# Two of VectorE's phases in a four-bit feed-forward stage change places

## The reference

```python
def fp4_quant_dequant(x):
    xb = x.reshape(shape[:-1] + (shape[-1] // BLOCK, BLOCK))          # BLOCK = 16
    scale = jnp.max(jnp.abs(xb), axis=-1, keepdims=True) / 6.0
    scale = jnp.maximum(scale, jnp.float32(1e-12))
    xn = xb / scale
    idx = jnp.searchsorted(_MID, jnp.abs(xn))
    q = _GRID[idx] * jnp.sign(xn) * scale
    return q.reshape(shape)

gate = fp4_linear(x, w_gate)
y = fp4_linear(x, w_up)
h = jax.nn.silu(gate) * y
return fp4_linear(h, w_down)
```

## Time and profile before

| | us |
|---|---|
| three runs: lowest, median, highest | 2645.53, 2656.07, 2657.33 |
| the profiled execution: its span | 2660.2 |
| of it TensorE busy | 2396.7 (90%) |
| VectorE busy | 1794.1 (67%) |
| ScalarE busy | 1297.3 (49%) |
| GpSimd busy | 710.9 (27%) |
| mean granted TensorE clock | 0.944 of full speed |

### The profile page before, as it was taken

How to read it: one execution, slowest core, us unless ns; L and a number is a source line. 1 busy time by engine, 2 the same in 40 slices (tenths; PEclk the granted TensorE clock), 3 DMA queues, 4 the chain that set the end, 5 groups by cost and what they waited for, 6 DMA issues and landing times. The chain is left out here.

```text
span 2660.2 us, 43690 instructions
## 1 busy us (share of the span) xinstructions
PE 2396.7 (90%) x15960; PEld 2204.5 (83%) x15960; DVE 1794.1 (67%) x3357; ACT 1297.3 (49%) x2026; POOL 710.9 (27%) x468
## 2 busy tenths in 40 slices
PE   6988896798999978999999999993999999499999
PEld 6887885788888877988988898883899999399998
DVE  5566665899999966566566566544667765777774
ACT  4344443334433324464454455444566665356555
POOL 1011011444444433123123023113244441211111
PEclk9999997899999998999999999975999999699999
DMA  5000000000000000000000000002000010000000
GB/s 171 0 0 0 0 0 18 2 1 0 0 0 0 1 1 17 13 8 12 16 4 12 16 6 9 16 9 64 17 24 24 16 48 1 34 19 30 24 24 32
DMA packets 42971, 45.69 MB, mean 17 GB/s; under 512 B 3088, under 2 KB 41872, under 8 KB 42640
## 3 DMA queue, kind: packets, MB, share of 16 engines
q1 hardware_dynamic: 42896, 44.69, 5.1%
HBM read 27.90 MB, written 16.78 MB: 17 GB/s over the span
## 5 line engine op out<-in xcount | busy, mean ns | idle before, releaser
L1842 DVE TENSOR_TENSOR m_a_lo<-m_a,m_a_hi 128x512 fp32r<-128x512 f32 x128 | 107.3, 839 | 126.4 <-ACT m_a_hi L1800 126.4
L1796 ACT ACTIVATE d_a<-d_ps_wide,d_b,d_w_gain 128x512 f32<-128x512 f32 x128 | 100.1, 782 | 136.7 <-PE d_ps_wide L271 134.4
L1269 POOL TENSOR_TENSOR p_kf<-p_kf,p_k_shift 128x1024 f32<-128x1024 f32 x64 | 119.4, 1904 | 155.4 <-DVE p_k_shift L1403 155.4
L1755 PE MATMUL m_ps_z<-m_w_hi,m_a_hi 128*128 128x256 f32 x512 | 147.4, 288 | 9.2 <-DVE m_w_lo L1821 9.2
L1796 ACT ACTIVATE m_a<-m_ps_wide,m_b 128x512 f32<-128x512 f32 x128 | 88.0, 688 | 121.3 <-PE m_ps_wide L271 121.2
L1755 PE MATMUL m_ps_z<-m_w_hi,m_a_lo 128*128 128x256 f32 x512 | 145.6, 284 | 0.0
L1755 PE MATMUL m_ps_z<-m_w_lo,m_a_hi 128*128 128x256 f32 x512 | 145.3, 284 | 0.0
L1755 PE MATMUL d_ps_z<-d_w_hi,d_a_hi 128*128 128x256 f32 x512 | 143.6, 280 | 1.1 <-DVE d_a_lo L1842 1.1
L1755 PE MATMUL d_ps_z<-d_w_lo,d_a_hi 128*128 128x256 f32 x512 | 143.4, 280 | 0.0
L1755 PE MATMUL d_ps_z<-d_w_hi,d_a_lo 128*128 128x256 f32 x512 | 142.6, 278 | 0.0
L1842 DVE TENSOR_TENSOR d_a_lo<-d_a,d_a_hi 128x512 fp32r<-128x512 f32 x128 | 85.8, 689 | 77.1 <-ACT d_a_hi L1800 72.5
(11 more groups left out here) (361 smaller groups left out, 8580.1 us busy)
## 6 DMA issues: line engine op xcount, KB each, us to landing
residual<-in_x SPq DMA_DIRECT2D x8, 1024.0 KB, 11.8
attn<-p_attn SPq DMA_DIRECT2D x32, 256.0 KB, 2.1
m_attn<-attn SPq DMA_DIRECT2D x16, 512.0 KB, 3.7
out<-residual SPq DMA_DIRECT2D x16, 512.0 KB, 2.9
raw_weights<-in_d_q SPq DMA_DIRECT2D x2, 1024.0 KB, 7.1
d_scale<-in_d_scale SPq DMA_DIRECT2D x2, 1024.0 KB, 5.3
raw_weights<-in_m_w1T SPq DMA_DIRECT2D x1, 1024.0 KB, 5.1
raw_weights<-in_m_w2T SPq DMA_DIRECT2D x1, 1024.0 KB, 7.5
```

The lines of the kernel that those rows point to most:

```text
L1269: pool.tensor_tensor(f, f, k_shift[:, i, :].unsqueeze(2).broadcast_to([P, HEADS, M]), ALU.subtract).then_inc(k_shifted, 1)
L1755: mm = pe.matmul(z, a, w[:, f, :], start=(f == 0 and k == 0 and j % 2 == 0), stop=(f == FC - 1 and k == 2), skip_group_check=True)
L1796: act.activation(self.a[f % RING][:, :], self.ps_wide[f % 2][:, :], self.func, bias=self.b1[:, f:f + 1], scale=gain(f))
L1842: dve.tensor_tensor(self.a2[1][:, f, :], self.a[f % RING][:, :], self.a2[0][:, f, :].bitcast(F32), ALU.subtract).then_inc(self.a_lo, 1)
```

## The change

In VectorE's list of phases the block scales of the next normalised tile and the second gate product change places. Nothing else is touched.

```diff
             pipeline(dve, N, [(8, add_down), (4, split_n), (7, split_h(0)), (3, round_n), (6, round_h), (5, multiply(0)),
-                              (7, split_h(1)), (2, scales_n), (5, multiply(1)), (5, scales_h)], SLOTS)
+                              (7, split_h(1)), (5, multiply(1)), (2, scales_n), (5, scales_h)], SLOTS)
```

## The result

The changed kernel took 2680.89 us (median of 4 runs, 2673.06 to 2691.84) against 2650.94 us of the kernel before (four runs, 2645.53 to 2657.33): the ratio estimated from the runs is **1.0107**, 95% interval 1.0069 to 1.0145. It is slower by 30 us; the forecast was 38.6 us more and a time of 2695, with a range from 2675 to 2714. The 2695 started from 2656.07, the median of three runs; with the fourth run the median of the kernel before is 5 us lower. The profiled execution took 2685.33 us and has a span of 2683.6.

A forecast was written before the change was run, and what follows sets the result against it. Two close limits, VectorE and a loop through the other engines with 0.92 us to spare, bound the kernel; scales in the loop (+21.0 us) plus 12 clock falls (17.6) gave +38.6 us, 2695 us, range 2675 to 2714.

The forecast's parts named there:

- The two close limits: Four-bit stage, kernel before: VectorE's own queue, 15.66 us a step, and a loop through other engines with 0.92 us to spare.
- the collision: VectorE's small product for the normalised tile's scales, blocked by GpSimd's restoring: 1.00 us instead of 0.18, 0.82 us a step.
- the loop: Gate product's scales through GpSimd's division, ScalarE's first SiLU and TensorE's up product back to VectorE: 14.79 us by itself.
- The wait at the gate product: VectorE's second gate product waits for TensorE's up product: from 0 to 1.65 us in an ordinary step.
- The price of the scales in the loop: Normalised tile's scales between up product and gate product's scales add 0.73 + 0.65 + 0.34 = 1.72 us a step.
- The signal gap behind the reciprocal: VectorE, from the reciprocal's end of the normalised tile's scales to the next instruction: 0.34 us, low bound 0.04.
- The uncontended small product: VectorE's small product in the normalised tile's scales, clear of GpSimd's restoring: 0.18 us, 0.65 to the reciprocal's end.
- The first step: Start of the stage's first counted gate-product scales, whose product already waited for TensorE: 1.72 us later.
- The falls of the clock: TensorE's clock falling to 1.2 GHz in 12 of 28 steps instead of 8, 1.47 us each, 17.6 us.
- The sum: Whole forecast: +19.3 us in 28 steps, 1.72 for the first start, 17.6 for falls: +38.6 us.
- VectorE is the bound: Rival, faster: collision's 0.82 us saved each step, 2633 us, if the up product is done when the split ends; chance 0.02.

The follow-up runs named there:

- the filled kernels: Unread TensorE matmuls added to each step where TensorE waits: ten in the changed kernel, ratio 1.0030; nine in the kernel before, ratio 0.9994.

## Why the prediction was right

**What bounds the kernel.** The two close limits were there. With the collision taken away VectorE's 15.66 became 14.84 and stopped at the loop's 14.79; with the scales in the loop the step became 16.13. The rows that told it were the last three steps, not the busy share.

**The wait at the gate product.** Forecast 0 to 1.65 us in every step; measured in all 28, in the step shown 1.46 us (from the split's end at 746.37 to 747.83), and some 3 us in a step with a fall.

**The price of the scales in the loop: 1.72 us, measured 1.34** (16.13 - 14.79). Two pieces of this term were too large. The signal gap behind the reciprocal is 0.16 us, not 0.34: I took over the gap ahead of a product with three waits, and now one wait stands there. That the number of waits makes the difference was not tested. And the reduction starts 0.81 us after the gate product, not 0.93 (748.64 against 747.83), since it waits for nothing of it. That makes 0.30; the way from the scales to the up product, 13.70 us against 13.78 in the last steps, makes the rest. The uncontended small product was right: 0.18, and 0.65 to the reciprocal's end; the rule of the Trainium skill (SBUF — State Buffer, "Who interferes with whom") held in every order tried: 0.18 us wherever GpSimd was free, 0.54 to 1.28 wherever it was not, and 0.46 instead of 0.21 for the gate product's small product in the one kernel where that met GpSimd.

**The first step.** Forecast 1.72 us, measured 2.33 - 0.92 = 1.41, for the same reason.

**The falls of the clock: 12 expected, 18 measured.** The direction was right, and the filled kernels show the cause that was argued. The size was a choice between two ends and was too low; 18 lies on the edge of the 5 to 18 that the forecast allowed, so that it came out inside is luck. Its price of 1.47 us was right (1.53).

**The sum.** In the 28 steps +19.3 without falls and 17.6 for them were forecast, 36.9; measured 8.68 (451.68 - 443.00) and 27.66 (479.34 - 451.68), together 36.34. So the stage came out as forecast because two terms were off in opposite directions by 10 us each, not because both were known: that is luck. The kernel's 30 us are less than the stage's 36 to 38: the stages that the edit does not touch differ between executions, by 7.8 and 6.7 us in the two profiled ones, and four runs of each do not average that out. On record are 46 later runs of the kernel before; they lie between 2634.9 us (granted clock 0.954) and 2663.1 (0.944). Which stages make this spread is not shown.

**The rivals.** "VectorE is the bound" had the right price and fell on its condition: the up product did not end with the split. Of the orders tried, only the one with GpSimd's order changed instead of VectorE's, the scales staying ahead of the gate product, earns that price, and it is the fastest kernel of this study (0.9897).

## What to carry to other kernels

When two engines hand a tile round in a loop, find the loop's own length where the work beside it is missing, here in the last steps, and ask of every moved phase where it stands: in the wait of the loop it costs nothing as long as it fits, behind the wait it costs its full length. A stall seen on a row is worth removing by moving the other engine's work when the stalled work already stands in a free place; then look what the moved work meets next. And count what an order leaves to spare: 0.92 us in a step had been paying more than half of every fall of TensorE's clock.

## What the runs showed of the hardware

Ten matmuls that nobody reads made the changed kernel's stage 27.7 us shorter: placed in TensorE's waits of 0.9 and 1.2 us, they kept the granted clock at 1.00 over 450 us, where it had fallen to its 1.2 GHz level in 18 of 28 steps. More idle time did not simply mean more falls: with GpSimd's order exchanged in the changed kernel TensorE waited longer, and in one piece a step (75.4 us in 28 waits, against 65.9 in 55), and its clock fell in 14 steps.
